# An attention and experts kernel: the gate as a tanh in the expert phase, six groups' output stage in the last thirteen attention blocks

## The chip, the cores and the metric

The kernel runs on one core of one Trainium2 chip. The metric is the device time of one execution in microseconds (us). The core has a matrix engine (TensorE, PE in the profile; its weight loads are PEld), a vector engine (VectorE, DVE), an activation engine (ScalarE, ACT), a general engine (GpSimd, POOL), and SyncE (SP), which issues the transfers between device memory and on-chip memory. Each engine works its own instructions strictly in order; between engines the order is kept by semaphores. TensorE writes into PSUM, which has eight banks of 128 x 512 floats.

## The reference, cut to what matters

```
x  = L0_attn_z                                  # 4 x 1024 tokens x 128
xn = layernorm(x)
zn = layernorm(xn) * ln_w + ln_b
q, k, v = split(zn @ W_qkv + b_qkv)             # 16 heads of 8 columns
p  = softmax(q k^T / sqrt(8))                   # 1024 x 1024 for each of 64 heads
s  = xn + concat(p @ v) @ W_proj + b_proj
w  = softmax over the 2 largest of (xn @ Wr + br), 8 experts
f  = sum_e w_e * (gelu(xn @ W1_e + b1_e) @ W2_e + b2_e)
out = x + s * silu(f)
```

## The kernel before, in words

The 4096 tokens are eight groups of 512 (`TG = 512`, `NG = 8`), two for each of the four sequences. Data of a group stand transposed: 128 model columns on the partitions, 512 tokens along them.

**The expert phase** goes over the eight groups; each has 32 slots (8 experts x 4 hidden chunks). In a slot TensorE multiplies chunk i up (L832 to L834, three matmuls, for a split in high and low parts), ScalarE applies the gelu (L716 and L719, or L710 for each fourth chunk), VectorE or GpSimd forms the low part (L1181, L612), and TensorE multiplies down (L848 to L856) three slots later. VectorE adds up the experts' shares (L1198) and closes a group with `total` (L1204), at slot 37 counted from the group's start, which is slot 5 of the next group; it writes `ffn`, the f of the reference. Beside this run the normalisation of the next group and the row maxima of the first eight pairs of heads (L867 on TensorE, L1237 on VectorE). After the last group eight more slots (`LAG`) drain what is left.

**The attention phase** goes over 256 blocks (`BLOCKS`): 32 pairs of heads, 8 blocks of 128 keys each. Block n has two score steps, 2n and 2n+1, each of two matmuls for one half of the queries (L927), into two PSUM areas in turn. ScalarE exponentiates 1024 columns for each (L753); `scores(s)` waits until the exponential of step s-2 is done. At the end of block n TensorE multiplies the probabilities of block n-2 with the values (`pv`, L947, eight instructions for four matmuls), into bank 4. Up to block 239 there are row maxima of later pairs too (`max_scores` L867, `row_max` L1219), in a ring of the banks 5, 6 and 7; from block 240 on these are done. When a pair is through, ScalarE copies its sums out (`o_copy`, L744), TensorE turns them (`o_t`, L960, four transposes, in the sixth block of the next pair), and VectorE divides by the softmax sums and writes `msa` (`head_out`, L1260 and L1265).

**The output stage** of a group is: turn `msa` (`msa_turn`, L973, four transposes), copy to `msaT` (`msa_copy`, L1273, VectorE), project (`project`, L981), add bias and xn (`sum_y`, L1279), multiply with the gate (`gate_y`, L1285 on VectorE, or L646 on GpSimd for groups 0 to 3), turn back (`y_turn`, L993), add x (`finish`, L1292), and store (SyncE). The gate is silu(f), eight activations (L763) after the last exponential. `msa_turn` and `project` of groups 0 to 5 stand in a table `ends` by half blocks. It starts at block `TAIL` = 254, so that two turns and one projection fall into the loop; the rest of the table is worked off behind it. Groups 6 and 7 need the last pair's `head_out`.

The order on each engine is written out by hand; no scheduler moves anything.

## Time and profile before

| what | us |
|---|---|
| device time, median of 3 runs (lowest, highest) | 1130.94 (1129.79, 1131.89) |
| device time of the profiled execution | 1131.14 |
| its span, first to last instruction | 1129.3 |
| TensorE busy (share of the span) | 1062.4 (94%) |
| VectorE busy | 896.3 (79%) |
| ScalarE busy | 847.7 (75%) |
| GpSimd busy | 365.0 (32%) |

The span is what the trace shows; the device time has 1.84 us more around it in this execution. Matmul ends are modelled, so the start of the next instruction tells more of what one costs than its duration does. Busy shares are averages over three stages: experts up to about 516 us, attention up to about 1100 us, and the output stage behind it.

### The profile page before, as it was taken

How to read it: one execution, taken by the hardware profiler on the slowest of the kernel's cores; microseconds unless marked ns; L12 is line 12 of the kernel's file. 1: busy time of each engine (PE TensorE's matmuls, PEld its weight loads, DVE VectorE, ACT ScalarE, POOL GpSimd, SP SyncE). 2: the span in 40 equal slices, each digit the busy share in tenths (PEclk: the TensorE clock that was granted, in tenths of full speed). 3: DMA queues.
4: the chain of work that ended last, by engine and by line, in shares of the span. 5: the costliest groups of instructions: out<-in, count | busy, mean ns of one | idle time of the engine just before them, and what ended most of it. 6: DMA issues, size and time to landing. Idle time of an engine off the chain costs nothing.

```text
span 1129.3 us, 17260 instructions
## 1 busy us (share of the span) xinstructions
PE 1062.4 (94%) x6041; PEld 438.8 (39%) x6041; DVE 896.3 (79%) x1567; ACT 847.7 (75%) x1133; POOL 365.0 (32%) x534
## 2 busy tenths in 40 slices
PE   5698999999999999999999999999999999999995
PEld 4475656566666666663122222222121212212123
DVE  7566778777768687666999999999999999999715
ACT  6575666566666666667988898888889898988982
POOL 3795656656666666453010001000000000000001
PEclk9899999999999999998999999999999999999998
DMA  4523131414141322223111112111211111111102
GB/s 144 150 83 84 61 86 29 117 34 118 32 114 33 102 51 64 75 72 92 45 44 44 39 35 56 32 45 29 58 31 44 40 48 45 30 44 30 30 1 75
DMA packets 84992, 67.42 MB, mean 60 GB/s; under 512 B 9277, under 2 KB 71402, under 8 KB 84906
## 3 DMA queue, kind: packets, MB, share of 16 engines
q1 hardware_dynamic: 84906, 66.32, 21.7%
q8 instruction: 48, 0.79, 0.3%
q14 instruction: 38, 0.31, 0.1%
HBM read 51.08 MB, written 15.20 MB: 59 GB/s over the span
## 4 chain that ended last, share of the span: by engine, by line
PE 53%; ACT 19%; DVE 6%; issue 4%; ACTq 0%; DVEq 0%; POOL 0%; POOLq 0%
ACT p_ring L753 17%; PE psum L947 13%; PE psum L927 11%; PE psum L867 6%; PE psum L832 4%; PE psum L848 3%; PE psum L834 3%; PE psum L833 3%; PE psum L856 2%; PE psum L853 2%; PE psum L854 2%; DVE neg_max_half L1237 2%; PE psum L960 2%; DVE neg_max_half L1219 1%; PE psum L981 1%
## 5 line engine op out<-in xcount | busy, mean ns | idle before, releaser
L753 ACT ACTIVATE p_ring<-psum 128x1024 f32<-128x1024 f32 x512 | 500.7, 1023 | 66.0 <-PE psum L927 62.3
L1219 DVE TENSOR_REDUCE neg_max_half<-psum 128x1 f32<-128x512 f32 x768 | 486.3, 684 | 38.1 <-PE psum L867 29.0
L867 PE MATMUL psum<-k_max_stack,q_max_stack 48*128 48x512 bf16 x1024 | 300.6, 386 | 15.7 <-DVE neg_max_half L1237 9.6
L927 PE MATMUL psum<-q_stack,k_stack 51*128 51x512 bf16 x1024 | 279.1, 383 | 12.9 <-ACT p_ring L753 3.7
L947 PE MATMUL psum<-p_ring,v_sb 128*9 128x512 f32 x2048 | 268.5, 597 | 0.4 <-ACT o_sb L744 0.4
L716 ACT ACTIVATE h_hi<-psum,cols 128x512 fp32r<-128x512 f32 x192 | 132.0, 688 | 152.1 <-PE psum L834 147.9
L612 POOL TENSOR_TENSOR h_lo<-h_split,h_hi 128x512 fp32r<-128x512 f32 x128 | 164.5, 1289 | 141.0 <-ACT h_split L719 139.2
L1237 DVE TENSOR_REDUCE neg_max_half<-psum 128x2 f32<-128x1024 f32 x128 | 156.5, 1222 | 60.6 <-PE psum L867 60.4
L927 PEld LDWEIGHTS psum<-q_stack,k_stack 51*128 51x128 bf16 x1024 | 60.3, 94 | 305.8 <-ACT p_ring L753 281.4
L568 POOL CAST neg_max_parts<-neg_max_rest 128x16 bf16<-128x16 f32 x32 | 6.7, 211 | 510.6 <-DVE neg_max_rest L1228 510.6
L719 ACT ACTIVATE h_split<-psum,cols 128x512 f32<-128x512 f32 x192 | 130.9, 682 | 0.0
L832 PE MATMUL psum<-xn_t_hi,w_hi 128*128 128x512 f32 x256 | 128.4, 502 | 1.2 <-DVE w_lo L292 1.2
L867 PEld LDWEIGHTS psum<-k_max_stack,q_max_stack 48*128 48x128 bf16 x1024 | 69.6, 93 | 116.6 <-issue 43.3
L834 PE MATMUL psum<-xn_t_lo,w_hi 128*128 128x512 f32 x256 | 102.1, 399 | 0.0
L833 PE MATMUL psum<-xn_t_hi,w_lo 128*128 128x512 f32 x256 | 101.7, 397 | 0.0
L1181 DVE TENSOR_TENSOR h_lo<-h_split,h_hi 128x512 fp32r<-128x512 f32 x64 | 53.7, 839 | 50.8 <-ACT h_split L719 50.8
L856 PE MATMUL psum<-h_lo,w_hi 128*128 128x512 f32 x192 | 77.2, 402 | 9.1 <-POOL h_lo L612 4.6
L853 PE MATMUL psum<-h_hi,w_hi 128*128 128x512 f32 x192 | 76.4, 398 | 0.0
L854 PE MATMUL psum<-h_hi,w_lo 128*128 128x512 f32 x192 | 76.0, 396 | 0.0
L603 POOL TENSOR_TENSOR acc<-acc,prod 128x512 f32<-128x512 f32 x48 | 65.8, 1371 | 15.0 <-DVE prod L1198 15.0
L947 PEld LDWEIGHTS psum<-p_ring,v_sb 128*9 128x9 f32 x2048 | 31.0, 88 | 92.4 <-issue 92.1
L848 PE MATMUL psum<-h_full,w_full 128*128 128x512 f32 x128 | 65.4, 592 | 0.0
(114 smaller groups left out, 920.4 us busy)
## 6 DMA issues: line engine op xcount, KB each, us to landing
expert_w_bc<-expert_w_dram SPq DMA_DIRECT2D x64, 256.0 KB, 4.9
k_rows_dram<-qk_parts SPq DMA_DIRECT2D x24, 256.0 KB, 3.0
q_max_stack<-q_rows_dram SPq DMA_DIRECT2D x64, 96.0 KB, 2.5
k_max_stack<-k_rows_dram SPq DMA_DIRECT2D x64, 96.0 KB, 2.5
q_stack<-q_rows_dram SPq DMA_DIRECT2D x64, 96.0 KB, 2.5
k_stack<-k_rows_dram SPq DMA_DIRECT2D x64, 96.0 KB, 2.5
q_rows_dram<-qk_parts SPq DMA_DIRECT2D x8, 384.0 KB, 2.6
xz<-in_L_attn_z_dram SPq DMA_DIRECT2D x8, 256.0 KB, 3.2
```

Source lines behind the costliest of these rows:

```text
L612: pool.tensor_tensor(hl[:, (g * HS + j) % HR, :], h32[:, (g * HS + j) % FR, :], hh[:, (g * HS + j) % HR, :].bitcast(F32), ALU.subtract)\
L716: act.activation(hh[:, (g * HS + j) % HR, :], up, ACT.Gelu, bias=col(C_B1 + i))\
L719: act.activation(h32[:, (g * HS + j) % FR, :], up, ACT.Gelu, bias=col(C_B1 + i))\
L753: act.activation(p_sb[:, n % PR, a, :, :].rearrange("p h t -> p (h t)"), scores_bank[s % 2], ACT.Exp, scale=SCALE).then_inc(S("P"), 1)
L832: pe.matmul(o, w1h[:, e, ws], G(xh, g), start=True, stop=False)
L833: pe.matmul(o, w1l[:, e, ws], G(xh, g), start=False, stop=False)
L834: pe.matmul(o, w1h[:, e, ws], G(xl, g), start=False, stop=True).then_inc(S("h"), 1)
L867: return pe.matmul(to, q_m[rows, slot, t * P:(t + 1) * P], k_m[rows, slot, c * TG:(c + 1) * TG], start=True, stop=True)
L927: i = pe.matmul(scores_bank[s % 2][:, hh * TG:(hh + 1) * TG], k_s[rows, slot, kt * P:(kt + 1) * P], q_s[rows, slot, a * TG:(a + 1) * TG], ...
L947: i = pe.matmul(o_bank[at:at + VR, :], v_sb[:, b * KT + kt, 2 * (p % PB) + hh, :], p_sb[:, n % PR, a, hh, :], start=(kt == 0), stop=(kt == ...
L1219: dve.tensor_reduce(mx[:, p % MXR, c, hh * NT + t:hh * NT + t + 1], ring_bank(("max", u)), AX.X, ALU.max, negate=True).then_inc(S("R"), 1)
L1237: dve.tensor_reduce(mx[:, p % MXR, c, :].rearrange("p (h t) -> p h t", h=2)[:, :, t], early_bank, AX.X, ALU.max, negate=True).then_inc(S(" ...
```

## The change

1. **The gate.** silu(f) is f/2 (1 + tanh(f/2)). A new step `gate` on ScalarE, at slot 38 of each group, writes tanh(f/2) to a new tile `gt`. A new step `gated` on VectorE, at slot 39, writes (gt + 1) f over `ffn`. The factor 1/2 moves into `finish`, now a scalar_tensor_tensor. The eight silu activations go, and so do the four products on GpSimd: `gate_y` is on VectorE for all groups. For the last group both steps stand in the eight draining slots, ahead of the attention loop.
2. **Where the output stage stands.** The table `ends` now starts at block 243 and has three steps a group over two and a half blocks, `msa_turn`, `project` (with `sum_y` and `gate_y`) and `y_turn` (with `finish`), between the two score steps of a block. Groups 0 to 5 are thus stored while attention runs; groups 6 and 7 stay behind it.
3. **Banks.** `msa_turn` goes to bank 5 for all groups but the last (bank 0), `project` to bank 7 (1), `y_turn` to bank 6 (2). The last `o_t` still goes to bank 4; those of pairs 29 and 30 go to bank 6, so `y_turn` waits until `head_out` of that pair is done, and `o_t` of pair 30 waits for `finish` of group 3.
4. **Behind the loop** the copies to `msaT` for groups 6 and 7 are on ScalarE, and VectorE does `sum_y` and `gate_y` of both, then both `finish`.

Line numbers of the changed kernel differ: scores L944, `pv` L964, `o_t` L982, `msa_turn` L997, `project` L1009, `y_turn` L1018.

TensorE in blocks 244 to 246, before:

```order
L927 MATMUL psum<-q_stack,k_stack 128x512 x4
L947 MATMUL psum<-p_ring,v_sb 9x512 x4
L927 MATMUL psum<-q_stack,k_stack 128x512 x2
L960 MATMUL psum<-ident,o_sb 128x128 x4
L927 MATMUL psum<-q_stack,k_stack 128x512 x2
L947 MATMUL psum<-p_ring,v_sb 9x512 x4
```

and in the changed kernel:

```order
L944 MATMUL psum<-q_stack,k_stack 128x512 x2
L1009 MATMUL psum<-msa_t,wp_sb 128x512
L944 MATMUL psum<-q_stack,k_stack 128x512 x2
L964 MATMUL psum<-p_ring,v_sb 9x512 x4
L944 MATMUL psum<-q_stack,k_stack 128x512 x2
L982 MATMUL psum<-ident,o_sb 128x128 x4
L1018 MATMUL psum<-ident,y 128x128 x4
L997 MATMUL psum<-ident,msa 128x128 x4
L944 MATMUL psum<-q_stack,k_stack 128x512 x2
L964 MATMUL psum<-p_ring,v_sb 9x512 x4
```

Behind the first score step of a block there is now a projection, or a turn back with the next group's turn; in block 245 (and 253) also `o_t`, right ahead of the `y_turn` that waits for its `head_out`.

ScalarE where the expert phase ends, before:

```order
L716 ACTIVATE h_hi<-psum,cols 128x512
L719 ACTIVATE h_split<-psum,cols 128x512
L710 ACTIVATE h_full<-psum,cols 128x512
L729 ACTIVATE neg_max_t<-psum 48x128
L753 ACT_TABLE_LOAD
L753 ACTIVATE p_ring<-psum 128x1024 x20
```

and in the changed kernel:

```order
L719 ACTIVATE h_full<-psum,cols 128x512
L745 ACTIVATE neg_max_t<-psum 48x128
L735 ACTIVATE gate_tanh<-ffn_t 128x512
L769 ACT_TABLE_LOAD
L769 ACTIVATE p_ring<-psum 128x1024 x20
L760 ACTIVATE o_sb<-psum 128x512
```

The tanh of the last group stands between the last gelu and the load of the exponential's table. The other seven stand among the gelus, with no table load of their own.

TensorE from the last values product on, before:

```order
L947 MATMUL psum<-p_ring,v_sb 9x512 x12
L981 MATMUL psum<-msa_t,wp_sb 128x512
L973 MATMUL psum<-ident,msa 128x128 x4
L981 MATMUL psum<-msa_t,wp_sb 128x512
...
L981 MATMUL psum<-msa_t,wp_sb 128x512
L960 MATMUL psum<-ident,o_sb 128x128 x4
L973 MATMUL psum<-ident,msa 128x128 x8
L981 MATMUL psum<-msa_t,wp_sb 128x512 x2
L993 MATMUL psum<-ident,y 128x128 x32
```

and in the changed kernel:

```order
L964 MATMUL psum<-p_ring,v_sb 9x512 x12
L982 MATMUL psum<-ident,o_sb 128x128 x4
L997 MATMUL psum<-ident,msa 128x128 x8
L1009 MATMUL psum<-msa_t,wp_sb 128x512 x2
L1018 MATMUL psum<-ident,y 128x128 x8
```

Five projections, four turns and six of the eight turns back have left this place.

```diff
--- before.py
+++ after.py
...
@@ -213,7 +214,8 @@
             halves, turns = block_items(n)
             for item in halves[0] + turns + halves[1]:
                 on_ring(item)
-        TAIL = BLOCKS - KT + O_TURN + 1
+        ENDS_FROM = BLOCKS - 2 * KT + 3
+        o_late = bank[6]
 
         EARLY_AT = [HT + 4 + (27 * m) // 16 for m in range(EARLY)]
         EARLY_DONE = [EARLY_AT[(p + 1) * 2 * NT - 1] for p in range(EARLY_PAIRS)]
...
@@ -247,9 +249,6 @@
         NROW = HT + E + 5
 
         BESIDE = NG - NG // B
-        POOL_GATES = range(2 * BESIDE // 3)
-        DVE_GATES = [g for g in range(NG) if g not in POOL_GATES]
-
         def col(i):
             return cols[:, i:i + 1]
 
...
             return t[:, g, :] if isinstance(g, int) else t[:, bass.ds(g, 1), :].rearrange("p a t -> p (a t)")
+
+        def msa_bank(g):
+
+            return bank[0 if g == NG - 1 else 5]
+
+        def project_bank(g):
+
+            return bank[1 if g == NG - 1 else 7]
+
+        def y_bank(g):
+
+            return bank[2 if g == NG - 1 else 6]
+
+        def out_bank(p):
+
+            return o_bank if p == PAIRS - 1 else o_late if p >= PAIRS - 3 else ring_bank(("oT", p))
 
         def split(i):
 
...
 
-            for k, g in enumerate(POOL_GATES):
-                wait(pool, "gate", 0, 0, g + 1)
-                wait(pool, "y", 0, 0, g + 1)
-                pool.tensor_tensor(y[:, g, :], y[:, g, :], ffn[:, g, :], ALU.mult).then_inc(S("yg_p"), 1)
-
-
...
                     return step
-                return {i: [gelu(i)] for i in range(HT)}
+
+                def gate():
+                    wait(act, "acc", g, E - 1, E - 1)
+                    wait(act, "gated", g, 1, 0)
+                    act.activation(gt[:, :], ffn[:, g, :], ACT.Tanh, scale=0.5).then_inc(S("gate"), 1)
+                plan = {i: [gelu(i)] for i in range(HT)}
+                plan[4 * E + 6] = [gate]
+                return plan
 
             def neg_max_t(p, early=False):
                 m_tr = (b5 if early else ring_bank(("mT", p)))[0:NM, 0:P // 2].bitcast(BF16)
...
 
-
-            for g in range(NG):
-                act.activation(ffn[:, g, :], ffn[:, g, :], ACT.Silu).then_inc(S("gate"), 1)
+            for g in range(BESIDE, NG):
+                act.wait_ge(S("tm"), g + 1)
+                act.wait_ge(S("tp"), g - 1)
+                act.activation(msaT[:, g % 2, :], msa_bank(g), ACT.Copy).then_inc(S("tmc_a"), 1)
 
 
         @block.tensor
...
                 pe.wait_ge(S("oe"), p + 1)
-                to = o_bank
-                if p + 1 < PAIRS:
+                to = out_bank(p)
+                if p < PAIRS - 3:
                     ring_free(pe, ("oT", p))
-                    to = ring_bank(("oT", p))
+                elif p == PAIRS - 3:
+                    pe.wait_ge(S("R"), EARLY + len(SINGLES))
+                    pe.wait_ge(S("mTc"), PAIRS)
+                    pe.wait_ge(S("od"), PAIRS - 3)
+                elif p == PAIRS - 2:
+                    pe.wait_ge(S("ty"), 4)
                 for j in range(TT):
                     i = pe.transpose(to[:, j * P:(j + 1) * P], o_sb[:, p % 2, j * P:(j + 1) * P], ident[:, :])
                 i.then_inc(S("ot"), 1)
...
                 if g == 0:
                     pe.wait_ge(S("R"), EARLY + len(SINGLES))
                     pe.wait_ge(S("mTc"), PAIRS)
-                    pe.wait_ge(S("od"), PAIRS - 1)
+                    pe.wait_ge(S("od"), PAIRS - 3)
                 wait(pe, "od", 0, 0, (g // 2 + 1) * PB)
-                wait(pe, "tmc", 0, 0, g - 1)
+                wait(pe, "tmc", 0, 0, min(g, BESIDE))
+                if g == NG - 1:
+                    pe.wait_ge(S("P"), 2 * BLOCKS)
                 for t in range(TT):
-                    m = pe.transpose(bank[5 + g % 2][:, t * P:(t + 1) * P], msa[:, g * TT + t, :], ident[:, :])
+                    m = pe.transpose(msa_bank(g)[:, t * P:(t + 1) * P], msa[:, g * TT + t, :], ident[:, :])
                 m.then_inc(S("tm"), 1)
 
             def project(g):
                 if g == 0:
                     pe.wait_ge(S("wp"), 16)
-                wait(pe, "tmc", 0, 0, g + 1)
-                wait(pe, "y", 0, 0, g)
-                pe.matmul(bank[7][:, :], wp_sb[:, :], msaT[:, g % 2, :], start=True, stop=True)\
+                if g < BESIDE:
+                    wait(pe, "tmc", 0, 0, g + 1)
+                else:
+                    wait(pe, "tmc_a", 0, 0, g + 1 - BESIDE)
+                if g < NG - 1:
+                    wait(pe, "y", 0, 0, g)
+                pe.matmul(project_bank(g)[:, :], wp_sb[:, :], msaT[:, g % 2, :], start=True, stop=True)\
                     .then_inc(S("tp"), 1)
 
             def y_turn(g):
-                if g in POOL_GATES:
-                    wait(pe, "yg_p", 0, 0, POOL_GATES.index(g) + 1)
-                else:
-                    wait(pe, "yg_v", 0, 0, DVE_GATES.index(g) + 1)
-                wait(pe, "ty", 0, 0, g + 1 - len(ring))
-                if g == 2:
-                    pe.wait_ge(S("y"), NG)
+                wait(pe, "yg", 0, 0, g + 1)
+                if g < NG - 1:
+                    wait(pe, "ty", 0, 0, g)
+                wait(pe, "od", 0, 0, PAIRS - 2 if g < 4 else PAIRS - 1)
                 for t in range(TT):
-                    m = pe.transpose(ring[g % len(ring)][:, t * P:(t + 1) * P], y[:, g, t * P:(t + 1) * P],
-                                     ident[:, :])
+                    m = pe.transpose(y_bank(g)[:, t * P:(t + 1) * P], y[:, g, t * P:(t + 1) * P], ident[:, :])
                 m.then_inc(S("tt"), 1)
 
 
             ends = {}
             for g in range(BESIDE):
-                ends.setdefault(2 * g, []).append(lambda g=g: msa_turn(g))
-                ends.setdefault(2 * g + 2, []).append(lambda g=g: project(g))
+                ends.setdefault(4 * g, []).append(lambda g=g: msa_turn(g))
+                ends.setdefault(4 * g + 2, []).append(lambda g=g: project(g))
+                ends.setdefault(4 * g + 4, []).insert(0, lambda g=g: y_turn(g))
 
             pe.wait_ge(S("h32"), NG * HS)
             pe.wait_ge(S("hf"), NG * E)
             for n in range(BLOCKS):
                 p, kt = divmod(n, KT)
                 halves, turns = block_items(n)
-                at = 2 * (n - TAIL)
+                at = 2 * (n - ENDS_FROM)
                 scores(2 * n, halves[0])
                 for kind, k in turns:
                     m_t(k) if kind == "mT" else o_t(k)
@@ -1020,13 +1045,13 @@
                     step()
             pv(BLOCKS - 2)
             pv(BLOCKS - 1)
-            for at in range(2 * (BLOCKS - TAIL), 2 * BESIDE + 2):
+            for at in range(2 * (BLOCKS - ENDS_FROM), 4 * BESIDE + 1):
                 for step in ends.get(at, []):
                     step()
             o_t(PAIRS - 1)
 
             for step in (msa_turn, project, y_turn):
-                for g in range(0 if step is y_turn else BESIDE, NG):
+                for g in range(BESIDE, NG):
                     step(g)
 
 
...
 
+                def gated():
+
+                    wait(dve, "gate", g, 1, 1)
+                    dve.scalar_tensor_tensor(ffn[:, g, :], gt[:, :], 1.0, ffn[:, g, :], ALU.add, ALU.mult)\
+                        .then_inc(S("gated"), 1)
+
                 plan = {4 * e + 7: [combine(e)] for e in range(E)}
                 plan[4 * E + 5] = [total]
+                plan[4 * E + 7] = [gated]
                 for i in range(HT):
                     if split(i) and by_vector(i):
                         plan.setdefault(i, []).append(low_h(i))
...
 
                 b, h0 = p // PB, 2 * (p % PB)
                 dve.wait_ge(S("ot"), p + 1)
-                turned = (ring_bank(("oT", p)) if p + 1 < PAIRS else o_bank)[:, :]\
-                    .rearrange("p (j h a r) -> p h a j r", h=2, a=2, r=VC)
+                turned = out_bank(p)[:, :].rearrange("p (j h a r) -> p h a j r", h=2, a=2, r=VC)
                 dve.reciprocal(rden[:, p % 2, :, :, :], turned[:, :, :, :, DH]).then_inc(S("rd"), 1)
                 dve.wait_ge(S("rd"), p + 1)
                 for hh in range(2):
@@ -1270,39 +1301,40 @@
             def msa_copy(g):
                 wait(dve, "tm", 0, 0, g + 1)
                 wait(dve, "tp", 0, 0, g - 1)
-                dve.tensor_copy(msaT[:, g % 2, :], bank[5 + g % 2][:, :]).then_inc(S("tmc"), 1)
+                dve.tensor_copy(msaT[:, g % 2, :], msa_bank(g)[:, :]).then_inc(S("tmc"), 1)
 
             def sum_y(g):
 
                 wait(dve, "tp", 0, 0, g + 1)
                 wait(dve, "xf", 0, 0, g + 1)
-                dve.scalar_tensor_tensor(y[:, g, :], bank[7][:, :], col(C_BP), y[:, g, :],
+                dve.scalar_tensor_tensor(y[:, g, :], project_bank(g)[:, :], col(C_BP), y[:, g, :],
                                          ALU.add, ALU.add).then_inc(S("y"), 1)
 
             def gate_y(g):
-                wait(dve, "gate", 0, 0, g + 1)
+                wait(dve, "gated", 0, 0, g + 1)
                 wait(dve, "y", 0, 0, g + 1)
-                dve.tensor_tensor(y[:, g, :], y[:, g, :], ffn[:, g, :], ALU.mult).then_inc(S("yg_v"), 1)
+                dve.tensor_tensor(y[:, g, :], y[:, g, :], ffn[:, g, :], ALU.mult).then_inc(S("yg"), 1)
 
             def finish(g):
                 if g == 0:
                     wait(dve, "tx", 0, 0, 16 * NG)
                 wait(dve, "tt", 0, 0, g + 1)
                 dst = x_out[:, g, :, :]
-                dve.tensor_tensor(dst, ring[g % len(ring)][:, :].rearrange("p (t d) -> p t d", d=D), dst, ALU.add)\
-                    .then_inc(S("ty"), 1)
+                dve.scalar_tensor_tensor(dst, y_bank(g)[:, :].rearrange("p (t d) -> p t d", d=D), 0.5, dst,
+                                         ALU.mult, ALU.add).then_inc(S("ty"), 1)
 
             ends = {}
             for g in range(BESIDE):
-                ends.setdefault(2 * g, []).append(lambda g=g: msa_copy(g))
-                ends.setdefault(2 * g + 2, []).append(lambda g=g: sum_y(g))
+                ends.setdefault(4 * g, []).append(lambda g=g: msa_copy(g))
+                ends.setdefault(4 * g + 2, []).append(lambda g=g: (sum_y(g), gate_y(g)))
+                ends.setdefault(4 * g + 4, []).insert(0, lambda g=g: finish(g))
 
             dve.wait_ge(S("vd"), NG)
             dve.memset(o_bank[:, :], 0.0).then_inc(S("o_zero"), 1)
             for n in range(BLOCKS):
                 halves, turns = block_items(n)
                 p, kt = divmod(n, KT)
-                at = 2 * (n - TAIL)
+                at = 2 * (n - ENDS_FROM)
                 if n in min_at:
                     half_min(min_at[n])
                 for _, u in halves[0]:
@@ -1316,20 +1348,15 @@
                     row_max(u)
                 for step in ends.get(at + 1, []):
                     step()
-            for at in range(2 * (BLOCKS - TAIL), 2 * BESIDE + 2):
+            for at in range(2 * (BLOCKS - ENDS_FROM), 4 * BESIDE + 1):
                 for step in ends.get(at, []):
                     step()
             head_out(PAIRS - 1)
             for g in range(BESIDE, NG):
-                msa_copy(g)
+                sum_y(g)
+                gate_y(g)
             for g in range(BESIDE, NG):
-                sum_y(g)
-            for g in range(NG):
-                if g in DVE_GATES:
-                    gate_y(g)
-                if g:
-                    finish(g - 1)
-            finish(NG - 1)
+                finish(g)
 
 
 # ---- launch: one core; inputs and outputs as the reference has them ----
```

## Rows read from the trace of the kernel before

**Rows 1.** Windows: length; busy PE, PEld, DVE, ACT, POOL; PE clock; DMA share; GB/s

```profile
1071.65:1100.59 28.94, 26.70 (x195) 6.64 (x191) 3.26 (x9) 25.74 (x28) 0.00 (x0) 1.00 0.00 1
1100.59:1129.30 28.71, 17.07 (x74) 9.64 (x74) 16.82 (x28) 6.16 (x10) 4.99 (x4) 0.88 0.26 74
```

**Rows 2.** Timeline, blocks 253 to 255: start, duration (us), engine, line, operation

```profile
1091.28 0.39 PE L927 MATMUL psum<-q_stack,k_stack 51*128 51x512 bf16 x2
...
1091.60 0.66 PE L960 MATMUL psum<-ident,o_sb 128*128 128x128 f32 x4
...
1092.19 0.39 PE L927 MATMUL psum<-q_stack,k_stack 51*128 51x512 bf16 x2
1092.29 0.26 DVE L1260 RECIPROCAL rden<-psum 128x16 f32<-128x16 f32 x1 [15.12 <-PE psum L960]
...
1094.39 0.39 PE L927 MATMUL psum<-q_stack,k_stack 51*128 51x512 bf16 x2
...
1095.69 0.39 PE L927 MATMUL psum<-q_stack,k_stack 51*128 51x512 bf16 x2
...
1096.01 1.13 PE L981 MATMUL psum<-msa_t,wp_sb 128*128 128x512 f32 x2
...
1096.97 0.60 PE L973 MATMUL psum<-ident,msa 128*128 128x128 f32 x4
...
1097.83 2.76 PE L947 MATMUL psum<-p_ring,v_sb 128*9 128x512 f32 x24
```

**Rows 3.** Timeline, behind the last exponential

```profile
1100.66 0.60 ACT L744 ACTIVATE o_sb<-psum 128x512 f32<-128x512 f32 x1 [1.69 <-PE psum L947]
...
1102.35 0.68 DVE L1273 COPY msa_t<-psum 128x512 f32<-128x512 f32 x1
...
1103.09 1.12 PE L981 MATMUL psum<-msa_t,wp_sb 128*128 128x512 f32 x2 [1.00 <-DVE msa_t L1273]
...
1104.25 0.75 DVE L1279 SCALAR_TENSOR_TENSOR y<-psum,cols,y 128x512 f32<-128x512 f32 x1 [1.22 <-PE psum L981]
1104.92 0.68 DVE L1273 COPY msa_t<-psum 128x512 f32<-128x512 f32 x1
...
1112.62 0.25 DVE L1260 RECIPROCAL rden<-psum 128x16 f32<-128x16 f32 x1
...
1113.30 0.86 PEld L973 LDWEIGHTS psum<-ident,msa 128*128 128x128 f32 x8 [1.20 <-DVE msa L1265]
...
1125.91 0.69 DVE L1292 TENSOR_TENSOR x_out<-psum,x_out 128x512 f32<-128x512 f32 x1 [0.53 <-PE psum L993]
```

**Rows 4.** Timeline, where the expert phase ends

```profile
516.68 1.28 ACT L753 ACT_TABLE_LOAD   x1
...
517.99 1.94 ACT L753 ACTIVATE p_ring<-psum 128x1024 f32<-128x1024 f32 x2
...
518.24 0.69 DVE L1204 TENSOR_TENSOR ffn_t<-acc,prod 128x512 f32<-128x512 f32 x1
...
519.43 1.22 DVE L1219 TENSOR_REDUCE neg_max_half<-psum 128x1 f32<-128x512 f32 x2
```

**Rows 5.** Timeline of TensorE, the first maximum of block 0 that waits

```profile
520.11 0.39 PE L867 MATMUL psum<-k_max_stack,q_max_stack 48*128 48x512 bf16 x1 [1.25 <-DVE neg_max_half L1219]
520.34 0.38 PE L927 MATMUL psum<-q_stack,k_stack 51*128 51x512 bf16 x1
```

**Rows 6.** Windows there, columns as in Rows 1

```profile
521.90:528.70 6.80, 6.80 (x32) 1.21 (x31) 5.41 (x9) 4.81 (x6) 0.00 (x0) 0.51 0.97 258
```

**Rows 7.** Timeline, ScalarE around slot 6 of the third group

```profile
157.91 0.68 ACT L719 ACTIVATE h_split<-psum,cols 128x512 f32<-128x512 f32 x1
158.73 0.69 ACT L716 ACTIVATE h_hi<-psum,cols 128x512 fp32r<-128x512 f32 x1
```

**Rows 8.** Timeline, VectorE at the same place

```profile
156.46 0.68 DVE L1204 TENSOR_TENSOR ffn_t<-acc,prod 128x512 f32<-128x512 f32 x1
...
159.91 1.23 DVE L1237 TENSOR_REDUCE neg_max_half<-psum 128x2 f32<-128x1024 f32 x1 [1.64 <-PE psum L867]
```

1 line of the change is left out of this document (added).

## The prediction

> **What bounds the kernel now.** I read the windows first. The last thirteen attention blocks and what follows are two stretches of nearly the same length, 28.94 and 28.71 us [rows 1]. In the first one ScalarE is busy for 25.74 us, TensorE for 26.70, VectorE for 3.26: there is no room to speak of on TensorE, and almost all of VectorE is free. In the second nothing is full: TensorE 17.07, VectorE 16.82, ScalarE 6.16 of 28.71. That stretch is one chain of hand-overs, and it is what the change attacks.
>
> Then the timeline of blocks 253 to 255, for what each piece costs TensorE. I take the distance from one start to the next, since the durations overlap [rows 2]: a score step 0.32 us (1091.28 to 1091.60); a `pv` 1.30 - 0.32 = 0.98 (1094.39 to 1095.69 less the score step); four transposes 0.59 (1091.60 to 1092.19); a projection 0.96 to the next start, with 1.13 as its duration, and I take 1.0; the last three `pv` together 2.76. A bare block thus holds 2 x 0.32 + 0.98 = 1.62 us of TensorE work, where the window gives 28.94 / 13 = 2.2 us. So TensorE has 0.6 us a block to give at most, some 2.7 us over the stretch once the two `o_t`, two turns and one projection that stand there already are counted, before each inserted instruction lengthens the block.
>
> **The last thirteen blocks.** From the first score of block 243 (1071.65) to the last `o_copy`, TensorE will have: 26 score steps x 0.32 = 8.32; twelve `pv` x 0.98 + 2.76 = 14.52; fourteen sets of four transposes (six `msa_turn`, six `y_turn`, two `o_t`) x 0.59 = 8.26; six projections x 1.0 = 6.0. Sum 37.10.
>
> Two waits come on top. In blocks 245 and 253 `y_turn` stands right behind `o_t` and must wait for `head_out` of the same pair, since they share bank 6; behind it in TensorE's queue stand the next turn, a score step and a `pv`. `o_t` to reciprocal takes 0.69 us (1091.60 to 1092.29 [rows 2]), reciprocal to the next TensorE work 0.68 (1112.62 to 1113.30 [rows 3]), together 1.37, of which 0.59 is `o_t` itself: 0.78 us, twice, 1.56.
>
> The other new waits I cost at nothing, and this is their cover. `y_turn` waits for projection to `sum_y` (1103.09 to 1104.25, 1.16), `sum_y` to `gate_y` (0.67, as 1104.25 to 1104.92) and `gate_y` to TensorE (0.74, as 1102.35 to 1103.09) [rows 3], 2.57 us; TensorE meanwhile has 1.0 + 0.32 + 0.98 + 0.32 = 2.62 us of its own. That is a margin of 0.05, so a miss is likely now and then, but a miss costs only the difference. The projection waits for the turn's copy with 0.7 us to spare. ScalarE needs about one microsecond for an exponential (25.74 / 26 [rows 1]) and one step comes from TensorE in 1.3 us and more on average (38.7 / 26 = 1.5), so it becomes the one that waits.
>
> So 37.10 + 1.56 = 38.66, and 0.07 to the start of `o_copy`: 38.73 us, against 1100.66 - 1071.65 = 29.01 before. **Cost: 9.7 us.** With the projection at 1.13 it is 10.5; with projections and transposes overlapping a little better than I count, 8.7.
>
> **Behind the last values product.** Before, from the start of the last `o_copy` to the end of the span: 1129.30 - 1100.66 = 28.64 us. After, the chain has these links [rows 3], where the transposes' hand-over is that of [rows 2]: `o_copy` to `o_t` 0.74; `o_t` to reciprocal 0.69; to `msa_turn` of group 6 0.68; to the copy 0.69; to the projection 0.74; to `sum_y` 1.16; then `gate_y` of group 6, `sum_y` and `gate_y` of group 7 in a row, three times 0.67; to its `y_turn` 0.74; to the last `finish` 0.69; from its start to the end of the span 1129.30 - 1125.91 = 3.39, and 0.07 more since it becomes a scalar_tensor_tensor (0.75 against 0.68). Sum: 0.74 + 0.69 + 0.68 + 0.69 + 0.74 + 1.16 + 2.01 + 0.74 + 0.69 + 3.46 = 11.60. **Gain: 17.0 us.** The silu's and the GpSimd products' own time is nothing in this: they ran beside the chain. What is late next is that same chain of two groups; it cannot go lower by more than the projection of group 7.
>
> **Where the expert phase ends.** The last tanh waits for `total` of the last group, which starts at 518.24, while the exponentials start at 517.99 today [rows 4]. The tanh can start 0.74 later, at 518.98; it takes 0.60 like the 512-column copy of [rows 3]; the table load takes 1.31 with its gap (516.68 to 517.99). The first exponential starts at about 520.9, 2.9 us late. VectorE's `gated` waits for the tanh as well, and the memset and the first maximum behind it in the queue come at 519.43 + 1.3. But TensorE idles there already: it sits until 520.11 for the first maximum and then issues the scores of block 1 at 520.34 [rows 5]. After the change that maximum lets it go at 521.4, and these scores need the first exponential's end, at about 521.9. **Cost: 1.5 us** (521.9 - 520.34), with 0 as the lower bound, if later waits swallow it, and 2.9 as the upper.
>
> What TensorE's clock does here is the uncertain part. After 1.25 us of idleness the granted clock was 0.51 from 521.90 to 528.70, that is the 1.2 GHz level [rows 6]. The idleness becomes 2.6 us. If the low stretch moves along with the work, nothing changes; if it lasts twice as long, 6.8 us more at half speed cost 3.4 us.
>
> The Trainium skill ("TensorE: Matmul & The Clock Gate", Part 1) says that the throttled state is the default and activity releases it, and so speaks against lengthening this idle stretch; by that rule the clock rival below would be the forecast.
>
> **Inside the expert phase.** Seven tanh and seven `gated` lie among other work. In the third group `total` starts at 156.46 [rows 8] and ScalarE is through with the gelu ahead of the tanh at 158.59 [rows 7], so the tanh does not wait; it would push the next gelu from 158.73 to about 159.1, on an engine that is busy for 75% of the span. `gated` fits into the 1.64 us that VectorE idles before 159.91 [rows 8]. I take 0.3 us in all, between 0 and 7 x 0.67 = 4.7 if every `gated` delayed the maximum that TensorE waits for.
>
> **The sum.** Span 1129.3 + 9.7 - 17.0 + 1.5 + 0.3 = 1123.8; with the 1.84 us around the span (1131.14 - 1129.3) 1125.6. The profiled execution lies 0.2 above the median of the three runs, so against the median I say **1125.5 us**, 5.4 below 1130.94.
>
> **The rivals.**
> - *The hand-overs are not hidden* (slower). TensorE waits at every projection and every `y_turn` in the last blocks as it does behind them today, 1.00 us before the projection at 1103.09 [rows 3]: twelve times 1.0 on top, 1137.5. It decides from the point where the chain of 2.57 us outgrows TensorE's own 2.62 by a whole link. Against it: VectorE is free there, 3.26 of 28.94 us [rows 1]. Chance 0.05.
> - *The longer idleness keeps the clock low for twice as long*: 3.4 more, 1128.9. For it: the row of the clock [rows 6]. Against it: behind the loop today TensorE idles in every group and the mean clock is still 0.88 [rows 1]. Chance 0.10.
> - *The clock falls behind the loop.* The new chain has idle links too; turns, projection and turn back on it at 1.2 GHz add about 2 us: 1127.5. Chance 0.12.
> - *The gate's two steps show in the expert phase*, 4.7 instead of 0.3: 1129.9. For it: TensorE is nearly full there and in order, and waits for VectorE's maxima. Against it: the idle 1.64 us. Chance 0.08.
> - *The late exponentials are absorbed* and the insertions are a little cheaper: 1.5 less, 1124.0. Chance 0.13.
> - *A table load costs more than its row.* In this trace the exponential starts 0.03 us behind the end of the load [rows 4]; if a drain of about the load's own length stood with it once the tanh has just run, the first exponential would be 1.3 us later, 1126.8. The Trainium skill ("ScalarE: Activation LUTs", What ACT_TABLE_LOAD costs) puts such a drain, 1380 ns, beside the load; the row does not show it. Chance 0.02.
>
> **How the numbers follow.** The forecast has 0.50; the six rivals have the other half. A measurement of this kernel tells about 0.2%, 2.3 us, from no change, so faster means below 1128.7. Faster: 0.50, 0.12, 0.13, 0.02 and half of the first clock rival, 0.05: 0.82. Within 0.2%: its other half and the expert phase, 0.13. Slower 0.05. The range runs from 1123.2 (all in-block costs at their low end) to 1129.4, which leaves out the slower case and the upper part of the expert one.
>
> **What the profile will show.** Right: thirteen blocks of about 38.7 us with TensorE busy throughout and ScalarE waiting for it; two waits of 0.8 us for `head_out` there; from the last `o_copy` to the end 11.6 us; the first exponential some 2.9 us later against the last gelu; maxima in the expert phase no later than before. The forecast falls if the blocks take over 41 us, or if attention without its last thirteen blocks is longer by over 3 us.

## The result and the profile after

The changed kernel takes 1129.1 us (median of 12 runs, 1127.43 to 1130.83) against 1130.85 for the kernel before in the same comparison (12 runs, 1128.8 to 1132.66). The ratio is 0.9982, with a 95% interval of 0.9973 to 0.9990: about 2 us faster, where 5.4 were forecast; 1129.1 lies at the upper edge of the forecast's range of 1123.2 to 1129.4. The profiled execution took 1128.79 us with a span of 1127.0.

I cut every trace at the same five marks and read the distances off the timelines. A is from the start of `total` of group 0 to `total` of group 7 (the expert phase); B from the last h_full activation to the first `o_copy` (its end and the first blocks of attention); C from there to the exponential of step 486; D from there to the last `o_copy` (the last thirteen blocks); E from there to the end. What lies ahead of A is left out: the first `total` came at 93.4 to 96.9 us in the traces of this study, whatever the kernel, so a single span says little. B starts 4.06 us before A ends, in every trace.

| us | A | B | C | D | E |
|---|---|---|---|---|---|
| before, first trace | 424.2 | 28.15 | 529.90 | 28.43 | 28.66 |
| before, second trace | 423.3 | 27.91 | 529.95 | 28.43 | 28.29 |
| changed, first trace | 426.4 | 30.47 | 530.17 | 38.26 | 11.81 |
| changed, second trace | 425.5 | 29.75 | 530.22 | 38.26 | 11.81 |
| mean difference | +2.2 | +2.1 | +0.3 | +9.8 | -16.7 |
| forecast | +0.3 | +1.5 | 0 | +9.7 | -17.0 |

(The forecast of D was for the time from the first score of block 243, 0.57 us ahead of the mark; it moves both kernels alike.) The two large terms came out as forecast, within 0.3 us each. The smaller ones, ahead of them, take back 4.6 of the 6.9 us that the two leave, where 1.8 were forecast.

Windows of the changed kernel over the last thirteen blocks and what follows, to set beside [rows 1]; the columns are the same:

```profile
1076.37:1115.19 38.82, 37.01 (x244) 12.22 (x240) 17.71 (x30) 27.48 (x28) 0.00 (x0) 1.00 0.15 42
1115.19:1127.00 11.81, 5.04 (x24) 2.79 (x24) 4.70 (x9) 1.68 (x3) 0.00 (x0) 0.85 0.16 44
```

TensorE is now busy for 37.0 of the 38.8 us (26.7 of 28.9 before), and ScalarE has the slack. The mean clock of 0.85 in the last row comes from the time behind the last matmul.

TensorE's timeline in blocks 244 to 247 (246 left out), to set beside [rows 2]:

```profile
1078.58 0.39 PE L944 MATMUL psum<-q_stack,k_stack 51*128 51x512 bf16 x2
1078.89 1.13 PE L1009 MATMUL psum<-msa_t,wp_sb 128*128 128x512 f32 x2
1079.95 0.39 PE L944 MATMUL psum<-q_stack,k_stack 51*128 51x512 bf16 x2
1080.27 1.04 PE L964 MATMUL psum<-p_ring,v_sb 128*9 128x512 f32 x8
1081.25 0.39 PE L944 MATMUL psum<-q_stack,k_stack 51*128 51x512 bf16 x2
1081.57 0.66 PE L982 MATMUL psum<-ident,o_sb 128*128 128x128 f32 x4
1083.06 0.63 PE L1018 MATMUL psum<-ident,y 128*128 128x128 f32 x4 [0.83 <-DVE msa L1296]
1083.52 0.60 PE L997 MATMUL psum<-ident,msa 128*128 128x128 f32 x4
1084.06 0.39 PE L944 MATMUL psum<-q_stack,k_stack 51*128 51x512 bf16 x2
...
1088.03 0.39 PE L944 MATMUL psum<-q_stack,k_stack 51*128 51x512 bf16 x2
1088.44 0.66 PE L1018 MATMUL psum<-ident,y 128*128 128x128 f32 x4
1088.94 0.60 PE L997 MATMUL psum<-ident,msa 128*128 128x128 f32 x4
1089.47 0.39 PE L944 MATMUL psum<-q_stack,k_stack 51*128 51x512 bf16 x2
```

A projection costs 1.06 us (1078.89 to 1079.95). The wait of `y_turn` for `head_out` is there in block 245, 0.83 us, and again in block 253. From 1088.03 to 1088.44 it is 0.41 us in place of 0.32: `y_turn` comes 0.09 us late; `gate_y`, which it waits for, starts 0.85 us behind `sum_y` and not 0.67.

VectorE's timeline behind the last `o_copy`, to set beside [rows 3]:

```profile
1119.75 0.75 DVE L1310 SCALAR_TENSOR_TENSOR y<-psum,cols,y 128x512 f32<-128x512 f32 x1 [2.56 <-PE psum L1009]
1120.60 0.69 DVE L1316 TENSOR_TENSOR y<-y,ffn_t 128x512 f32<-128x512 f32 x1
1121.21 0.74 DVE L1310 SCALAR_TENSOR_TENSOR y<-psum,cols,y 128x512 f32<-128x512 f32 x1
1122.06 0.69 DVE L1316 TENSOR_TENSOR y<-y,ffn_t 128x512 f32<-128x512 f32 x1
```

`gate_y` follows `sum_y`, whose result it waits for, after 0.85 us, not 0.67. That puts three links 0.30 us over the forecast (2.31 us from 1119.75 to 1122.06, against 2.01), and E at 11.81 instead of 11.60.

Now the end of the expert phase, where [rows 4] and [rows 5] were taken; ScalarE, VectorE and GpSimd, then TensorE:

```profile
521.09 0.63 ACT L735 ACTIVATE gate_tanh<-ffn_t 128x512 f32<-128x512 f32 x1 [2.30 <-DVE ffn_t L1229]
521.73 1.28 ACT L769 ACT_TABLE_LOAD   x1
523.03 1.94 ACT L769 ACTIVATE p_ring<-psum 128x1024 f32<-128x1024 f32 x2
```

```profile
520.36 0.69 DVE L1229 TENSOR_TENSOR ffn_t<-acc,prod 128x512 f32<-128x512 f32 x1
521.75 1.26 DVE L1234 SCALAR_TENSOR_TENSOR ffn_t<-gate_tanh,ffn_t 128x512 f32<-128x512 f32 x1 [0.69 <-ACT gate_tanh L735]
523.11 0.48 DVE L1333 MEMSET psum<- 128x512 f32 x1
523.51 4.80 DVE L1251 TENSOR_REDUCE neg_max_half<-psum 128x1 f32<-128x512 f32 x8
```

```profile
521.20 1.26 POOL L653 TENSOR_TENSOR y<-xn_t_hi,xn_t_lo 128x512 f32<-128x512 f32 x1 [2.56 <-DVE ffn_t L1229]
```

```profile
524.19 0.60 PE L884 MATMUL psum<-k_max_stack,q_max_stack 48*128 48x512 bf16 x1 [3.20 <-DVE neg_max_half L1251]
```

`total` starts at 520.36, the tanh 0.73 us later, and the first exponential 2.67 us after `total`, as worked out. But `gated` takes 1.26 us where I had 0.67, beside an addition of GpSimd that ends at 522.46. The first maximum comes at 523.51, 3.15 us behind `total` instead of 1.19, and TensorE idles 3.20 us instead of 1.25: the maximum lets it go 3.83 us behind `total` (524.19), and the next scores follow at 4.23. The forecast had the end of the first exponential as what ends this wait, 3.66 us behind `total`.

In the expert phase the product stands at slot 7. In the third group, the place of [rows 8], first on VectorE and then on GpSimd:

```profile
159.17 0.69 DVE L1234 SCALAR_TENSOR_TENSOR ffn_t<-gate_tanh,ffn_t 128x512 f32<-128x512 f32 x1 [0.87 <-ACT gate_tanh L735]
159.94 1.23 DVE L1269 TENSOR_REDUCE neg_max_half<-psum 128x2 f32<-128x1024 f32 x1
```

```profile
159.24 3.03 POOL L627 TENSOR_TENSOR h_lo<-h_split,h_hi 128x512 fp32r<-128x512 f32 x2 [0.18 <-issue]
```

There the product starts 0.07 us ahead of GpSimd's pair of h_lo and takes 0.69 us, and the maximum behind it starts 3.46 us behind `total` (156.48), as before. In the fourth group:

```profile
221.52 1.22 DVE L1269 TENSOR_REDUCE neg_max_half<-psum 128x2 f32<-128x1024 f32 x1
223.60 1.67 DVE L1234 SCALAR_TENSOR_TENSOR ffn_t<-gate_tanh,ffn_t 128x512 f32<-128x512 f32 x1 [0.87 <-ACT gate_tanh L735]
225.19 1.21 DVE L1269 TENSOR_REDUCE neg_max_half<-psum 128x2 f32<-128x1024 f32 x1
```

```profile
223.45 2.97 POOL L627 TENSOR_TENSOR h_lo<-h_split,h_hi 128x512 fp32r<-128x512 f32 x2
```

VectorE waits 0.87 us for the tanh again, but now the pair of h_lo is ahead by 0.15 us, and the product takes 1.67 us. The maximum behind it starts 4.28 us behind `total` (220.91 to 225.19); in the kernel before it is 3.45 us in this group (220.39 to 223.84), behind the same idle 1.64 us as in [rows 8]. That is 0.8 us late, and so it is in the fifth and the sixth group.

TensorE does not wait for that maximum, though, but for a later one, whose result comes 9 to 10 us behind `total`. In the fourth group, in the kernel before and in the changed one:

```profile
229.74 0.39 PE L867 MATMUL psum<-k_max_stack,q_max_stack 48*128 48x512 bf16 x2 [0.65 <-DVE neg_max_half L1237]
```

```profile
230.85 0.39 PE L884 MATMUL psum<-k_max_stack,q_max_stack 48*128 48x512 bf16 x2 [1.24 <-DVE neg_max_half L1269]
```

Between the two maxima VectorE has no idle time above 0.04 us, so what is late at the first is still late at the second. In the third group, where the first one is in time, the second is 0.5 us late all the same: GpSimd's pair ends later, and a normalisation step of VectorE (L1122) beside it takes 1.27 us in place of 0.78.

### The profile page after: what moved, and what is told of

It reads as the page before. It is cut to its first block, busy times and chain, and to the rows that moved or that the text cites. A ratio compares the mean times of both kernels' runs of the same rounds, so it can differ in the third digit from the quotient of the medians.

```text
span 1127.0 us, 17277 instructions
## 1 busy us (share of the span) xinstructions
PE 1060.0 (94%) x6041; PEld 437.3 (39%) x6041; DVE 904.1 (80%) x1577; ACT 849.7 (75%) x1134; POOL 362.6 (32%) x530
## 4 chain that ended last, share of the span: by engine, by line
PE 53%; ACT 18%; DVE 6%; issue 4%; ACTq 0%; DVEq 0%; POOL 0%; POOLq 0%
ACT p_ring L769 16%; PE psum L964 14%; PE psum L944 11%; PE psum L884 6%; PE psum L849 4%; PE psum L851 3%; PE psum L850 3%; PE psum L865 3%; DVE neg_max_half L1269 2%; PE psum L873 2%; PE psum L870 2%; PE psum L871 2%; PE psum L982 2%; DVE neg_max_half L1251 1%; ACT o_sb L760 1%
## 5 line engine op out<-in xcount | busy, mean ns | idle before, releaser
L884 PE MATMUL psum<-k_max_stack,q_max_stack 48*128 48x512 bf16 x1024 | 301.1, 386 | 21.0 <-DVE neg_max_half L1269 12.9
L944 PE MATMUL psum<-q_stack,k_stack 51*128 51x512 bf16 x1024 | 279.7, 384 | 11.2 <-ACT p_ring L769 2.4
L964 PE MATMUL psum<-p_ring,v_sb 128*9 128x512 f32 x2048 | 268.4, 597 | 0.2 <-ACT o_sb L760 0.2
L627 POOL TENSOR_TENSOR h_lo<-h_split,h_hi 128x512 fp32r<-128x512 f32 x128 | 166.9, 1307 | 140.6 <-ACT h_split L728 138.6
L944 PEld LDWEIGHTS psum<-q_stack,k_stack 51*128 51x128 bf16 x1024 | 60.3, 94 | 307.1 <-ACT p_ring L769 268.5
L884 PEld LDWEIGHTS psum<-k_max_stack,q_max_stack 48*128 48x128 bf16 x1024 | 69.4, 93 | 121.2 <-issue 43.3
L1206 DVE TENSOR_TENSOR h_lo<-h_split,h_hi 128x512 fp32r<-128x512 f32 x64 | 51.4, 803 | 53.0 <-ACT h_split L728 53.0
L964 PEld LDWEIGHTS psum<-p_ring,v_sb 128*9 128x9 f32 x2048 | 31.0, 88 | 92.5 <-issue 89.8
```

Of the source, the lines that this page charges most:

```text
L627: pool.tensor_tensor(hl[:, (g * HS + j) % HR, :], h32[:, (g * HS + j) % FR, :], hh[:, (g * HS + j) % HR, :].bitcast(F32), ALU.subtract)\
L884: return pe.matmul(to, q_m[rows, slot, t * P:(t + 1) * P], k_m[rows, slot, c * TG:(c + 1) * TG], start=True, stop=True)
L944: i = pe.matmul(scores_bank[s % 2][:, hh * TG:(hh + 1) * TG], k_s[rows, slot, kt * P:(kt + 1) * P], q_s[rows, slot, a * TG:(a + 1) * TG], ...
L964: i = pe.matmul(o_bank[at:at + VR, :], v_sb[:, b * KT + kt, 2 * (p % PB) + hh, :], p_sb[:, n % PR, a, hh, :], start=(kt == 0), stop=(kt == ...
```

## The experiments

Each kernel differs from the changed one, or from the one before, by the edit shown. Theory G says that the missing three microseconds are what the gate's two steps cost among the experts and at their end; the rival R, that the expert phase simply differs that much between executions.

**Both kernels again (b1, b2).** No edit.

> The kernel before, unchanged, for a second trace. Stretches are cut at the start of the last h_full activation (end of the gelus), the first exponential, the first o_copy, and the last o_copy. In the first trace they end at 514.2, 518.0, 542.3 and 1100.7 us. Theory G (the missing time is in the gate's steps among the experts): the last h_full again at 514.2 within 0.5. Rival R (the expert phase differs by that much between executions of one program): it comes more than 1 us away, towards the 516.3 of the changed kernel.

> The changed kernel, unchanged, for a second trace. Theory G: last h_full again at 516.3 within 0.5 us, first exponential 6.7 us later, thirteen last blocks 38.3 from the exponential of step 486 to the last o_copy, end 11.8 us later. Rival R: the last h_full at another place, near 514.2. Device time 1129 for both.

Their rows are the second traces in the table. By my expectation as it was written, the last h_full at 514.2 and 516.3 within 0.5 us, the first held (514.4) and the second did not (517.0): what lies ahead of the first `total` moves too much for that mark. By the distance A, 424.2 and 423.3 stand against 426.4 and 425.5. Device time of the second: 1128.95 us, ratio 0.9981 (0.9970 to 0.9992), the same result as the first time.

**The gate alone, in the kernel before (b3).**

```diff
+                def gate():
+                    wait(act, "acc", g, E - 1, E - 1)
+                    wait(act, "gated", g, 1, 0)
+                    act.activation(gt[:, :], ffn[:, g, :], ACT.Tanh, scale=0.5).then_inc(S("gate"), 1)
+                plan[4 * E + 6] = [gate]
...
+                plan[4 * E + 7] = [gated]
...
-            for g in range(NG):
-                act.activation(ffn[:, g, :], ffn[:, g, :], ACT.Silu).then_inc(S("gate"), 1)
```

> The kernel before with part 1 of the change alone: tanh and product among the experts, no silu at the end, the output stage where it was and the GpSimd products kept. Theory G: the costs of the expert phase (2.1 us) and of its end (2.3 us) are all there and nothing is gained, since the silus ran beside the chain: 4 us slower than before, about 1135, last h_full at 516.3. Rival R: the expert phase costs 0.3 and its end 1.5, about 1132.7, last h_full near 514.5.

1135.79 us in the median, ratio to before 1.0035 (1.0023 to 1.0048), that is 4 us slower by the ratio. A 426.8, B 29.94, C 530.25, D and E as before (28.43, 28.29). The silus really cost nothing where they stood, and the gate costs 3.0 us in A against the mean of the two traces of the kernel before, 1.9 in B, 0.3 in C.

**The move alone (b4).** The gate factor is left out of the output.

```diff
-                plan[4 * E + 6] = [gate]
...
-                plan[4 * E + 7] = [gated]
...
-                wait(dve, "gated", 0, 0, g + 1)
```

> The changed kernel without tanh and product (the gate factor is left out: ffn enters the output ungated). Parts 2 to 4 alone. Theory G: expert phase as before (last h_full 514.2, first exponential 3.8 us later), blocks and tail as in the changed kernel: some 4.4 us faster than it, about 1124.6. Rival R: it gains only the predicted 1.8 us, about 1127.3. A third theory, that the move itself gives less than its traces say, would leave it at 1129.

1124.58 us, ratio 0.9936 (0.9924 to 0.9948): 7.2 us faster than before by the ratio. A 423.0, B 28.02, C 529.96, all as before; D 37.97, E 11.66. The move gives what its traces say, and theory G holds: the shortfall is the gate's. R falls. A part of D and E is the gate's as well, 0.29 and 0.15 us: `gate_y`, which has one wait less here, follows `sum_y` after 0.79 us instead of 0.85.

**Tanh or product (c1, c2).** Which of the two steps delays the experts?

```diff
# c1: the tanh without the product, nor the waits for it
...
-                plan[4 * E + 7] = [gated]
...
# c2: the product without the tanh
-                plan[4 * E + 6] = [gate]
...
-                    wait(dve, "gate", g, 1, 1)
+                    wait(dve, "acc", g, E - 1, E - 1)
+                    wait(dve, "gz", 0, 0, 1)
...
+                pool.memset(gt[:, :], 0.0).then_inc(S("gz"), 1)
```

Neither kernel has the gate in its output: c1 leaves the factor out, and in c2 it is 1, from a tile of zeros.

> The changed kernel with the eight tanh but without the product (the gate factor is left out of the output). Against the kernel without either (b4, 1124.6): theory V (the expert phase pays through VectorE, whose product delays the maxima) says total of group 0 to total of group 7 stays at about 423 us; theory S (it pays through ScalarE's queue) says 426. At the end of the expert phase both say last h_full to first exponential 6.7 us, since the tanh waits for total, and last h_full to first o_copy 1.5 to 2 us longer than b4's 28.0. V: device time 1126.3; S: 1129.

> The changed kernel with the eight products on VectorE, each right behind its own total and the maximum between them, but without the tanh (the second factor is a tile of zeros, written once, so the output has f in place of silu). Theory V: total 0 to total 7 is 426 as in the changed kernel, the products take 1.3 to 1.7 us where GpSimd reads at the same time; last h_full to first exponential back to 3.8, to first o_copy some 0.7 us over 28.0. Theory S: total 0 to total 7 is 423. V: 1127.5 to 1128; S: 1125.5.

c1: 1125.24 us, ratio 0.9955 (0.9939 to 0.9970); A 424.2, B 29.45. c2: 1125.99 us, ratio 0.9957 (0.9944 to 0.9971); A 425.1, B 29.06. Both lie between what the two theories said. The distance A itself scatters by 1.2 us among traces without either step, so I cut it once more, at every `total`, into seven intervals:

| us | first | second | third | fourth | last three | all but the first |
|---|---|---|---|---|---|---|
| neither step (before twice, b4, c3, c4) | 61.15 to 62.40 | 63.94 | 62.53 | 62.75 | 172.6 | 361.77 to 362.07 |
| tanh alone (c1) | 62.07 | 63.96 | 62.65 | 62.95 | 172.5 | 362.09 |
| product alone (c2) | 61.85 | 64.33 | 62.85 | 63.16 | 172.9 | 363.25 |
| both (changed twice, b3, d1, d2, d3) | 61.70 to 62.81 | 64.44 | 63.12 | 63.41 | 172.8 | 363.62 to 363.94 |

Nearly all of the scatter is in the first interval. In the other six the means are 361.86 us without and 363.77 with both steps: 1.9 us, of which the product alone has 1.4 and the tanh alone 0.2. The first interval adds 0.5 us in the mean, within its scatter. So theory V is nearer. And the cost stands in three intervals, 0.5 to 0.7 us in each; the last three have almost none. TensorE does not wait at that place there, though in the first of the three the maximum is as late (8.68 us behind `total` against 8.08). One expectation failed in an instructive way: the products in c2 do not take 1.3 to 1.7 us. VectorE in the fourth group of c2:

```profile
221.07 1.22 DVE L1270 TENSOR_REDUCE neg_max_half<-psum 128x2 f32<-128x1024 f32 x1
222.21 0.69 DVE L1235 SCALAR_TENSOR_TENSOR ffn_t<-gate_tanh,ffn_t 128x512 f32<-128x512 f32 x1
223.91 1.23 DVE L1270 TENSOR_REDUCE neg_max_half<-psum 128x2 f32<-128x1024 f32 x1 [1.01 <-PE psum L884]
```

Without the tanh to wait for, the product is done before GpSimd's pair of h_lo starts, and takes 0.69 us. It is the wait for the tanh that pushes it onto them. The maximum that TensorE waits for starts 8.07 us behind `total` in this group in the kernel before, 8.19 in c1, 8.39 in c2 and 8.66 in the changed kernel; the wait grows by nearly the same steps, 0.65, 0.76, 0.98, 1.24 us. The place where all of this reaches TensorE is its wait for a maximum. The lines of L867 (L884, L883) between 100 and 516 us, with TensorE's idle time ahead of them and its cause, for the kernel before, c1, c2 and the changed kernel:

```profile
L867 PE MATMUL psum<-k_max_stack,q_max_stack 48*128 48x512 bf16 x250 | 48.7, 386 | 9.6 <-DVE neg_max_half L1237 9.4
```

```profile
L883 PE MATMUL psum<-k_max_stack,q_max_stack 48*128 48x512 bf16 x250 | 48.7, 386 | 10.2 <-DVE neg_max_half L1267 10.2
```

```profile
L884 PE MATMUL psum<-k_max_stack,q_max_stack 48*128 48x512 bf16 x250 | 48.7, 386 | 11.0 <-DVE neg_max_half L1270 11.0
```

```profile
L884 PE MATMUL psum<-k_max_stack,q_max_stack 48*128 48x512 bf16 x250 | 48.7, 386 | 12.2 <-DVE neg_max_half L1269 12.0
```

9.6, 10.2, 11.0, 12.2 us: the same order as A. (In the second trace of the changed kernel it is 11.6.)

**Product and GpSimd kept apart (d1).** At the end of the experts the overlap can be taken away without touching anything else.

```diff
             pool.wait_ge(S("acc"), NG * (E - 1))
+            pool.wait_ge(S("gated"), NG)
```

> The changed kernel, with GpSimd's first addition of the attention phase held back until the last product on VectorE is done, so that the two no longer overlap. In the traces of the changed kernel that product took 1.26 us and 0.69 where GpSimd was idle. Theory P (an operation of VectorE that reads two tiles waits while GpSimd works): it takes 0.69 here and last h_full to first o_copy is 0.6 us shorter, 29.2; device time 1128.4. Rival: 1.26 again, it is the wait for the tanh or the transfers that lengthen it.

The last product on VectorE, and GpSimd's addition, in d1:

```profile
520.87 0.69 DVE L1230 TENSOR_TENSOR ffn_t<-acc,prod 128x512 f32<-128x512 f32 x1
522.25 0.69 DVE L1235 SCALAR_TENSOR_TENSOR ffn_t<-gate_tanh,ffn_t 128x512 f32<-128x512 f32 x1 [0.69 <-ACT gate_tanh L736]
523.05 0.48 DVE L1334 MEMSET psum<- 128x512 f32 x1
523.45 4.20 DVE L1252 TENSOR_REDUCE neg_max_half<-psum 128x1 f32<-128x512 f32 x7
```

```profile
523.12 1.26 POOL L654 TENSOR_TENSOR y<-xn_t_hi,xn_t_lo 128x512 f32<-128x512 f32 x1 [3.97 <-DVE ffn_t L1235]
```

0.69 us, and the first maximum 2.58 us behind `total` instead of 3.15. It was the overlap, and theory P holds. B is 29.40, against 29.75 and 30.47. That is 1.4 us over the kernel before, and so is c1, without a product, at 29.45: in both, the next scores come 3.75 us behind `total`, when the first exponential is done, as the forecast had it. Device time 1128.25 us, ratio 0.9984 (0.9975 to 0.9993): not to be told from the changed kernel, which 0.6 us in one place could not be.

**The last group's gate moved (d3).** Its tanh stands behind the first `o_copy`, its product on GpSimd, which has gaps of 20 us there.

```diff
...
+                if n == 11:
+                    wait(act, "acc", 0, 0, NG * (E - 1))
+                    wait(act, "gated", 0, 0, NG - 1)
+                    act.activation(gt[:, :], ffn[:, NG - 1, :], ACT.Tanh, scale=0.5).then_inc(S("gate"), 1)
...
+                    pool.wait_ge(S("gate"), NG)
+                    ch.mark(pool.tensor_scalar(gt[:, :], gt[:, :], 1.0, None, ALU.add))
+                    ch.end()
+                    pool.tensor_tensor(ffn[:, NG - 1, :], ffn[:, NG - 1, :], gt[:, :], ALU.mult)\
+                        .then_inc(S("gated_p"), 1)
```

> The changed kernel with tanh and product of the last group alone moved, the tanh behind the first o_copy into the twelfth attention block, the product to GpSimd, which is idle there. Expert phase as in the changed kernel (total 0 to total 7 at 426 us), its end as before (last h_full to first exponential 3.8, to first o_copy 28.0): 2.0 us less, 1127.0. If the last group's pair costs only what the prediction said, 1127.5.

1126.0 us, ratio 0.9964 (0.9952 to 0.9977), where 1127.0 was expected. B 28.08, A still 425.4. All that the end of the experts had lost is back. The exponential's table serves the tanh too: no second load stands in front of it.

**The whole gate moved to the last blocks (c3), and the turn ahead of the turn back (c4, d2).**

```diff
# c3: the tanh of group g behind the first exponential of block 243 + 2g, its product in the second half
+                    if tanh_at is not None and a == 0:
+                        gate(tanh_at)
...
+            for g in range(BESIDE + 1):
+                ends.setdefault(4 * g + 1, []).append(lambda g=g: gated(g))
# c4 and d2, on TensorE (and finish likewise on VectorE)
-                ends.setdefault(4 * g + 4, []).insert(0, lambda g=g: y_turn(g))
+            for g in range(BESIDE):
+                ends.setdefault(4 * g + 4, []).append(lambda g=g: y_turn(g))
```

c4 is c3 with the second edit, d2 the changed kernel with the second edit alone.

> The changed kernel with tanh and product taken out of the expert phase and put beside the output stage: tanh of group g behind the first exponential of block 243 + 2g, its product on VectorE in that block's second half, those of group 7 behind the last exponential. If the missing time is what the gate cost among the experts, this has all of it back: expert phase and its end as in b4, thirteen blocks at 38.3 us, since ScalarE idles 0.3 us a score step there and VectorE more, end 11.8: 1124.6. If ScalarE or VectorE turns late in the blocks by 0.3 us a group, 1126.5.

> As c3, and the next group's turn is issued ahead of the turn back, on TensorE and on VectorE. In blocks 245 and 253 the turn then fills 0.59 us of the 0.83 us that TensorE waits for head_out: 2 x 0.59 = 1.2 us less, 1123.4, thirteen blocks at 37.1. Rival: the copy of the turn comes ahead of finish, and the wait only moves; no difference to c3.

> The changed kernel with the next group's turn ahead of the turn back, nothing else. As c4 against c3: the thirteen blocks 37.1 us from the exponential of step 486 to the last o_copy in place of 38.25, device time 1127.9. If c4's gain came from something else, 1129.

c3: 1123.18 us, ratio 0.9933 (0.9921 to 0.9946). A 423.8, B 28.09, C 529.89, D 38.24: A, B and C as without the gate, D as in the changed kernel. All eight products take 0.68 or 0.69 us, GpSimd being idle. ScalarE in block 247 of c3, a tanh in what was a wait:

```profile
1082.73 1.02 ACT L773 ACTIVATE p_ring<-psum 128x1024 f32<-128x1024 f32 x1 [0.33 <-PE psum L951]
1083.65 0.62 ACT L760 ACTIVATE gate_tanh<-ffn_t 128x512 f32<-128x512 f32 x1
1084.17 1.02 ACT L773 ACTIVATE p_ring<-psum 128x1024 f32<-128x1024 f32 x1
```

c4: 1122.2 us, ratio 0.9926 (0.9914 to 0.9939), 8.4 us faster than the kernel before by the ratio and the lowest time of the study. From c3 its device time cannot be told; the trace tells it, D 37.10 against 38.24. TensorE in block 245 of c4:

```profile
1076.12 0.66 PE L989 MATMUL psum<-ident,o_sb 128*128 128x128 f32 x4
1076.61 0.60 PE L1004 MATMUL psum<-ident,msa 128*128 128x128 f32 x4
1077.61 0.63 PE L1025 MATMUL psum<-ident,y 128*128 128x128 f32 x4 [0.40 <-DVE msa L1297]
1078.17 0.39 PE L951 MATMUL psum<-q_stack,k_stack 51*128 51x512 bf16 x2
```

The turn fills the wait, of which 0.40 us stays. From the score ahead of `o_t` to the one behind the turns it was 2.81 us (1081.25 to 1084.06) and is 2.37 (1075.80 to 1078.17); the late `y_turn` of the other blocks is gone as well. d2 has the same D, 37.10, by itself: 1126.95 us, ratio 0.9978 (0.9969 to 0.9987). In device time that cannot be told from 0.9982; in the trace it is 1.15 us.

## Why the prediction was right in its large terms and wrong in the sum

1. **What bounds the kernel.** Right. TensorE alone set the last thirteen blocks, and two groups' hand-overs the end.
2. **The thirteen blocks**, 9.7 us forecast, 9.8 measured. The pieces were off by little and both ways: a projection 1.06 instead of 1.0, the two waits 0.83 instead of 0.78, the turn pairs cheaper (`y_turn` and `msa_turn` together 1.03 us, 1088.44 to 1089.47, instead of 1.18), and `y_turn` 0.09 late in most blocks, because `gate_y` waits 0.85 us for `sum_y`.
3. **The end**, 17.0 forecast, 16.7 measured. The three links of `gate_y` and `sum_y` took 2.31 us and not 2.01.
4. **The end of the experts**, 1.5 forecast, 2.1 measured. The first exponential was 2.9 us late as worked out. The term that was too small is `gated`: 0.67 taken, 1.26 measured, since GpSimd adds beside it. With it the first maximum, and not the first exponential, ended TensorE's wait. d1, with the product at 0.69, has 1.4 us; d3 shows that the whole loss belongs to the last group's pair.
5. **Inside the expert phase**, 0.3 forecast, 2.2 measured in the table, 1.9 without the first interval: the step that failed. I set the idle 1.64 us of one group against a product of 0.67 and took the rest as hidden. In that very group the product did fit, 0.69 us behind a wait of 0.87 for the tanh, and the maximum behind it came in time. Three things were not in the comparison. In the groups after it GpSimd's h_lo start 0.15 us ahead of the product, and it takes 1.67 us. In the third group, where the product is ahead, GpSimd's pair ends later, and the normalisation step beside it is longer instead. And the idle time that counts is not the one just ahead: TensorE waits for a maximum that VectorE starts 8 us behind `total`, at the end of work without a gap, 0.5 to 0.6 us late now. The bound of 4.7 was worked out from the right engine, but with 0.08 as its chance.
6. **The rivals.** "The gate's two steps show in the expert phase" was the one that came about, at half its price: only three of the seven intervals are longer beyond their scatter. The clock rival came about in part: where both steps of the last group stand at the end of the experts, the half-speed stretch was 10.24 us long in two of five traces (the first of the changed kernel and d2) and 6.83 in the other three. The two have a B of 30.5 us; of the others, b2 and b3 have 29.8 and 29.9, and d1, whose product is shorter too, 29.4. So its price was about 0.7 us and not 3.4, by these few traces; in the two, the stretch began 1.5 us before TensorE's idleness ended. The clock did not fall on the chain behind the loop of the changed kernel, only behind its last matmul; in the first trace of the kernel before it did fall there (1122.5), which is why its E is 0.37 us above the second's. The table load took 1.28 us, and the next activation followed 0.02 us behind it: no drain showed. The hand-overs in the blocks stayed hidden but for 0.09 us. The late exponentials were not absorbed.
7. **C**, 0.3 us, is there in every trace with a tanh among the experts and in none without. I have no cause for it, and it stays open. So does the first interval of A, which scatters by over 1 us whatever the kernel. Of the 1.9 us in the others, 0.3 are left beside tanh and product alone. The product of 1.67 us is what the two steps together have and neither has alone, but no run takes the overlap away among the experts, as d1 does behind them: that the 0.3 is its price is likely and not shown.

How large the miss is: 1.9 us in A, 0.6 in B, 0.3 each in C and in the end, 0.1 in D, 3.2 together, which leads from the forecast 5.4 to the measured 2.
